# The last layer of a two-layer perceiver kernel: another split of the first block's convolution, its rows written by ScalarE's queue, and sums, gate product and closing addition at later places in the long last stage

## The reference

```python
# Mamba block, on x = layernorm(X) as tokens of 256 features; 512 inner channels, 16 states
xz = x @ in_proj_w.T + in_proj_b
x_main, z = split(xz, 2)
xc = silu(causal_conv(x_main, conv_w, 4 taps per channel) + conv_b)
ssm = xc @ x_proj_w.T + x_proj_b          # 33 rows: B (16), C (16), one step size
delta = softplus(ssm[..., -1:])
A = -exp(A_log)
for t in tokens:                          # per sequence, channel and state
    h = exp(A * dt) * h + dt * B_t * x_t
    y = sum_n(h * C_t) + D * x_t
y = (y * silu(z)) @ out_proj_w.T + out_proj_b
x = X + layernorm(y + x) * gamma + beta
# experts, on layernorm(x): the kernel adds all 8 experts, scaled by one gate value per token
out = (sum over experts of (gelu(xf @ w1 + b1) @ w2 + b2)) * norm_g
x = x + out
```

## Time and profile before

| what | value |
|---|---|
| median of 3 runs | 1706.67 us |
| lowest and highest | 1701.71 and 1714.98 us |
| profiled execution, its own time | 1697.53 us |
| its span, first to last instruction | 1695.7 us |
| busy over the span: TensorE, VectorE, ScalarE, GpSimd | 1370.2, 1219.3, 1073.7, 772.5 us |
| mean granted TensorE clock, share of full speed | 0.89 |
| transfers, all on SP's queue | 211.88 MB, mean 125 GB/s |

### The profile page before, as it was taken

How to read it: one execution, slowest core, us unless ns; L and a number is a source line. 1 busy time by engine, 2 the same in 40 slices (tenths; PEclk the granted TensorE clock), 3 DMA queues, 4 the chain that set the end, 5 groups by cost and what they waited for, 6 DMA issues and landing times. The chain is left out here.

```text
span 1695.7 us, 33885 instructions
## 1 busy us (share of the span) xinstructions
PE 1370.2 (81%) x12684; PEld 780.3 (46%) x12684; DVE 1219.3 (72%) x2296; ACT 1073.7 (63%) x1901; POOL 772.5 (46%) x842
## 2 busy tenths in 40 slices
PE   5999447978769977788884578995988889799898
PEld 4545224655544435555552222341444445345566
DVE  3599799972348866677765688999899899895200
ACT  2677345543354547777764367876998898794553
POOL 2355000000043434343440067766888788887443
PEclk9999767989869978789896789996999899899999
DMA  7497200000106656787741398787894475470000
GB/s 266 145 357 302 106 0 0 1 1 0 70 25 237 198 114 114 138 127 126 133 67 37 78 244 204 211 225 191 200 217 114 116 177 138 105 180 8 1 13 13
DMA packets 152695, 211.88 MB, mean 125 GB/s; under 512 B 107247, under 2 KB 112303, under 8 KB 139600
## 3 DMA queue, kind: packets, MB, share of 16 engines
q1 hardware_dynamic: 152532, 209.70, 47.9%
HBM read 154.85 MB, written 31.75 MB: 110 GB/s over the span
## 5 line engine op out<-in xcount | busy, mean ns | idle before, releaser
L2865 POOL TENSOR_TENSOR c_st<-c_st,c_c_rep 128x1024 f32<-128x1024 f32 x128 | 301.9, 2358 | 118.8 <-DVE c_st L2978 118.7
L2978 DVE TENSOR_TENSOR_SCAN c_st<-mf_dA,mf_u_ps 128x512 f32<-128x512 f32 x256 | 310.1, 1211 | 4.0 <-ACT mf_dA L3090 4.0
L2806 PE MATMUL mf_eh<-c_early,c_experts 128*128 128x512 f16 x768 | 196.3, 394 | 27.9 <-POOL c_early L2884 16.9
L2888 POOL TENSOR_TENSOR c_early<-c_early 128x512 f16<-128x512 f32 x128 | 148.5, 1161 | 108.9 <-ACT c_early L3107 108.7
L2827 PE MATMUL mf_ey<-c_experts,c_early 128*128 128x256 f16 x1536 | 192.8, 277 | 0.0
L2972 DVE TENSOR_TENSOR mf_u_ps<-c_st,mf_b_ps 128x512 f32<-128x512 f32 x256 | 177.6, 694 | 11.5 <-DVE c_st L2978 0.5
L2827 PEld LDWEIGHTS mf_ey<-c_experts,c_early 128*128 128x128 f16 x1536 | 152.3, 99 | 49.7 <-issue 5.0
L3090 ACT ACTIVATE mf_dA<-c_dt,c_neg_a 128x496 f32<-128x496 f32 x256 | 160.3, 697 | 0.7
L3104 ACT ACTIVATE c_early<-mf_eh,c_vecs 128x512 f16<-128x512 f32 x128 | 88.0, 688 | 106.7 <-PE mf_eh L2806 106.2
L2732 PE MATMUL mf_y_ps<-c_st,c_consts 128*32 128x512 f32 x512 | 107.3, 654 | 50.4 <-POOL c_st L2865 33.1
L259 POOL TENSOR_TENSOR c_parts<-mg_ln_hT,c_parts 128x512 f16<-128x512 f32 x8 | 9.1, 1157 | 296.8 <-ACT c_parts L250 296.8
(11 more groups left out here) (546 smaller groups left out, 2759.4 us busy)
## 6 DMA issues: line engine op xcount, KB each, us to landing
c_st<-xs SPq DMA_DIRECT2D x64, 1024.0 KB, 7.3
a_ctx_t<-in_ctx_t SPq DMA_DIRECT2D x16, 1024.0 KB, 9.1
a_ctx_n<-in_ctx_n SPq DMA_DIRECT2D x16, 1024.0 KB, 8.1
cqs<-a_whole_rows SPq DMA_DIRECT2D x16, 512.0 KB, 6.7
mo_raw<-in_l_w SPq DMA_DIRECT2D x16, 512.0 KB, 4.1
ws<-mo_split SPq DMA_DIRECT2D x32, 256.0 KB, 2.6
c_cq<-cqs SPq DMA_DIRECT2D x16, 512.0 KB, 5.1
c_experts<-ws SPq DMA_DIRECT2D x32, 256.0 KB, 7.7
```

The lines of the kernel that those rows point to most:

```text
L2806: m = e.matmul(bank("hidden", n)[:, :], w1[q][w][:, j, f * P:(f + 1) * P], parts[b % 2][x][:, j, :], start=(j == 0 and w + x == 0), stop=( ...
L2865: e.tensor_tensor(half(u, h), half(u, h), over(c_rep[u // UNITS % 2][:, :], [P, 2, BT], 1), ALU.mult).then_inc(hcs("done"), 1)
L2888: e.tensor_tensor(hid[n % HIDS][1][:, :], g[n % 2][:, :], hid[n % HIDS][0][:, :], ALU.subtract).then_inc(los("done"), 1)
L2978: e.tensor_tensor_scan(st[u % RING][:, j, :], dA[:, n % AHEAD, :], u_ps[j % 2][:, :], 0.0, ALU.mult, ALU.add).then_inc(hs("done"), 1)
```

## The change

In the inner stage:
- `ON_V` is 2. VectorE convolves tiles 0 and 1; TensorE convolves tile 3 into `conv_ps` and tile 2 into `row_ps`. The silus and the row products go in the order 0, 3, 1, 2 (`KEPT`). The sums of the rows go into `conv_ps`, the step column into `row_ps`, the spread steps into `conv_ps`.
- VectorE makes the diagonals of tiles 2 and 3 and normalises the other twelve tiles ahead of its convolutions; the copies of block 1's transposes move ahead of the short chain. TensorE's transposes of block 1 move ahead of its convolutions.
- ScalarE copies the first features ahead of the root of the other tiles, and takes an exponential of a dummy value after the last silu.
- ScalarE's queue stores the rows right behind the activation that keeps them, waits for them and fetches them back replicated, ahead of its wait for the spread steps. SP does none of this.
- The fetches of state tiles 1 to 3 are the first transfers of SP in the last stage.

In the last stage, for steps from 23 on: `sums` stands behind both pairs of hidden and combine; `finish` stands behind the third scan and not the first. In all steps `gate` stands behind the second `weigh`, and `final(b - 1)` stands behind the first scan of the step after (two tiles later).

```diff
--- before.py
+++ after.py
@@ -2251,7 +2251,8 @@
                 drain(n)
 
 
-ON_V = DC - 1
+ON_V = 2
+KEPT = (0, DC - 1, 1, ON_V)
 
 
 def l1_inner(nc, c):
@@ -2266,6 +2267,7 @@
         xn_ps = [ps(f"xn_ps{j}") for j in range(CJ)]
         in_ps = [ps(f"in_ps{q}") for q in range(DC)]
         conv_ps, row_ps = ps("conv_ps"), ps("row_ps")
+        sum_ps = conv_ps
         acc = [sb(f"acc{u}", [P, BT]) for u in range(ON_V)]
         lg, na, ez, wz, lz, dz, mz, step = (sb(f"dt_{k}", [P, KT_]) for k in
                                             ("lg", "na", "ez", "wz", "lz", "dz", "mz", "step"))
@@ -2293,12 +2295,6 @@
                 e.dma_start(c.d["xs"][0, :, :, j, :].rearrange("q r t -> r q t"), c.xc[T * j:T * j + T, :, :]).then_inc(x_out, 16)
             e.wait_ge(x_out, 4 * 16)
             fetch_states(e, c, 0)
-            e.wait_ge(rows_kept, 1)
-            e.dma_start(c.d["ssm"][:, 0:BT], c.ssm[0:2 * NS, :]).then_inc(ssm_out, 16)
-            e.wait_ge(ssm_out, 16)
-            replicate_rows(e, c, 0)
-            for u in range(1, RING):
-                fetch_states(e, c, u)
             e.wait_ge(loaded, 3 * 16)
 
         @block.gpsimd
@@ -2314,7 +2310,7 @@
                     if i == 1:
                         e.wait_ge(kept_rows, CJ)
                     elif i:
-                        e.wait_ge(xs, DC)
+                        e.wait_ge(xs, (i - 2) * CJ + j + 1)
                     to = turn_banks[(max(i - 1, 0)) * CJ + j]
                     for k in range(KT_):
                         t = e.transpose(to[:, k * P:(k + 1) * P], c.xn[:, i * KT_ + k, j * P:(j + 1) * P], c.ident[:, :])
@@ -2328,27 +2324,28 @@
                     m = e.matmul(in_ps[q][:, :], c.w_x[:, j, q * P:(q + 1) * P], c.hT[:, j, 0:BT],
                                  start=(j == 0), stop=(j == CJ - 1))
                 m.then_inc(x_t, 1)
-            e.wait_ge(diag_made, TAPS)
-            e.wait_ge(xs, DC)
-            for k in range(TAPS):
-                m = e.matmul(conv_ps[:, :], c.diag[:, ON_V * TAPS + k, :], c.xm[:, ON_V, :, k:k + T],
-                             start=(k == 0), stop=(k == TAPS - 1))
-            m.then_inc(conv_t, 1)
-            for q in range(DC):
-                at = (ON_V, 0, 1, 2)[q]
-                e.wait_ge(silus, q + 1)
-                m = e.matmul(row_ps[0:NR, :], c.w_rows[:, at, :], c.xc[:, at, :], start=(q == 0), stop=(q == DC - 1))
+            turn(1)
+            e.wait_ge(diag_made, (DC - ON_V) * TAPS)
+            for q, to in ((DC - 1, conv_ps), (ON_V, row_ps)):
+                e.wait_ge(xs, DC)
+                for k in range(TAPS):
+                    m = e.matmul(to[:, :], c.diag[:, q * TAPS + k, :], c.xm[:, q, :, k:k + T],
+                                 start=(k == 0), stop=(k == TAPS - 1))
+                m.then_inc(conv_t, 1)
+            for q, at in enumerate(KEPT):
+                e.wait_ge(silus, max(q + 1, 2))
+                m = e.matmul(sum_ps[0:NR, :], c.w_rows[:, at, :], c.xc[:, at, :], start=(q == 0), stop=(q == DC - 1))
             m.then_inc(rows_t, 1)
             e.wait_ge(rows_kept, 1)
             for k in range(KT_):
-                m = e.matmul(conv_ps[:, k:k + 1], c.ssm[2 * NS:NR, k * P:(k + 1) * P], c.ones[2 * NS:NR, 0:1],
+                m = e.matmul(row_ps[:, k:k + 1], c.ssm[2 * NS:NR, k * P:(k + 1) * P], c.ones[2 * NS:NR, 0:1],
                              start=True, stop=True)
             m.then_inc(lg_t, 1)
-            for i in range(1, BLOCKS):
+            for i in range(2, BLOCKS):
                 turn(i)
             e.wait_ge(stepped, 1)
             for k in range(KT_):
-                m = e.matmul(row_ps[:, k * P:(k + 1) * P], step[:, k:k + 1].broadcast_to([P, P]), c.ident[:, :],
+                m = e.matmul(conv_ps[:, k * P:(k + 1) * P], step[:, k:k + 1].broadcast_to([P, P]), c.ident[:, :],
                              start=True, stop=True)
             m.then_inc(spread, 1)
 
@@ -2389,19 +2386,26 @@
                         o = e.scalar_tensor_tensor(a, x, w, a, ALU.mult, ALU.add)
                         o.then_inc(*(own() if k < TAPS - 1 else (conv, 1)))
 
+            def copy_turned(i):
+                for j in range(CJ):
+                    e.wait_ge(turned, i * CJ + j + 1)
+                    e.tensor_copy(c.hT[:, j, i * BT:(i + 1) * BT], turn_banks[(i - 1) * CJ + j][:, :]).then_inc(moved, 1)
+
             first, others = list(range(KT_)), list(range(KT_, TILES))
             statistics(first)
             normalised(first, 1)
             statistics(others)
-            taps_of(ON_V)
+            for q in range(ON_V, DC):
+                taps_of(q)
+            normalised(others, 2)
             for q in range(ON_V):
                 convolve(q)
-            normalised(others, 2)
             e.wait_ge(ready, 1)
             e.tensor_scalar(c.neg_a[:, :], c.neg_a[:, :], -1.0, None, ALU.mult).then_inc(made, 1)
+            copy_turned(1)
             e.wait_ge(lg_kept, 1)
             e.scalar_tensor_tensor(na[:, :], lg[:, :], -1.0, lg[:, :], ALU.mult, ALU.min).then_inc(negated, 1)
-            for q in range(ON_V - 1):
+            for q in range(ON_V):
                 taps_of(q)
             e.wait_ge(exped, 1)
             e.tensor_scalar(wz[:, :], ez[:, :], 1.0, None, ALU.add).then_inc(summed, 1)
@@ -2420,11 +2424,8 @@
             e.tensor_tensor(lz[:, :], lz[:, :], ez[:, :], ALU.mult).then_inc(*own())
             e.wait_ge(*own.now())
             e.scalar_tensor_tensor(step[:, :], lg[:, :], 0.0, lz[:, :], ALU.max, ALU.add).then_inc(stepped, 1)
-            taps_of(ON_V - 1)
-            for i in range(1, BLOCKS):
-                for j in range(CJ):
-                    e.wait_ge(turned, i * CJ + j + 1)
-                    e.tensor_copy(c.hT[:, j, i * BT:(i + 1) * BT], turn_banks[(i - 1) * CJ + j][:, :]).then_inc(moved, 1)
+            for i in range(2, BLOCKS):
+                copy_turned(i)
             e.wait_ge(moved, (BLOCKS - 1) * CJ)
 
         @block.scalar
@@ -2439,30 +2440,37 @@
 
             e.activation(c.neg_a[:, :], c.vec["A_log"], ACT.Exp).then_inc(ready, 1)
             root(list(range(KT_)))
-            root(list(range(KT_, TILES)))
             for j in range(CJ):
                 e.wait_ge(turned, j + 1)
                 e.activation(c.hT[:, j, 0:BT], xn_ps[j][:, :], ACT.Copy).then_inc(kept_rows, 1)
+            root(list(range(KT_, TILES)))
             e.wait_ge(cleared, 1)
             for q in range(DC):
                 e.wait_ge(x_t, q + 1)
                 e.activation(c.xm[:, q, :, TAPS - 1:], by_batch(in_ps[q][:, :]), ACT.Identity,
                              bias=bias[:, q:q + 1]).then_inc(xs, 1)
-            e.wait_ge(conv_t, 1)
-            keep_conv(conv_ps, ON_V)
-            for q in range(ON_V):
-                e.wait_ge(conv, q + 1)
-                keep_conv(acc[q], q)
+            for q in KEPT:
+                if q < ON_V:
+                    e.wait_ge(conv, q + 1)
+                    keep_conv(acc[q], q)
+                else:
+                    e.wait_ge(conv_t, DC - q)
+                    keep_conv(conv_ps if q == DC - 1 else row_ps, q)
+            e.activation(ez[:, :], lx.std[:, 0:KT_], ACT.Exp, scale=-1.0)
             e.wait_ge(rows_t, 1)
-            e.activation(c.ssm[:, :], row_ps[0:NR, :], ACT.Identity, bias=c.sm["xp_b"]).then_inc(rows_kept, 1)
+            e.activation(c.ssm[:, :], sum_ps[0:NR, :], ACT.Identity, bias=c.sm["xp_b"]).then_inc(rows_kept, 1)
+            e.wait_ge(rows_kept, 1)
+            e.dma_start(c.d["ssm"][:, 0:BT], c.ssm[0:2 * NS, :]).then_inc(ssm_out, 16)
             e.wait_ge(lg_t, 1)
-            e.activation(lg[:, :], conv_ps[:, 0:KT_], ACT.Copy).then_inc(lg_kept, 1)
+            e.activation(lg[:, :], row_ps[:, 0:KT_], ACT.Copy).then_inc(lg_kept, 1)
             e.wait_ge(negated, 1)
             e.activation(ez[:, :], na[:, :], ACT.Exp).then_inc(exped, 1)
             e.wait_ge(summed, 1)
             e.activation(lz[:, :], wz[:, :], ACT.Ln).then_inc(logged, 1)
+            e.wait_ge(ssm_out, 16)
+            replicate_rows(e, c, 0)
             e.wait_ge(spread, 1)
-            e.activation(c.dt[:, 0:BT], row_ps[:, :], ACT.Copy).then_inc(dt_kept, 1)
+            e.activation(c.dt[:, 0:BT], conv_ps[:, :], ACT.Copy).then_inc(dt_kept, 1)
 
 
 RING, AHEAD, HIDS, LAG = 4, 10, 6, 3
@@ -2691,6 +2699,8 @@
                 e.wait_ge(*added.at("done", b * KT_ + KT_ - 1))
                 e.dma_start(c.d["out"][:, rows(b), :], c.X[:, rows(b), :]).then_inc(stored, 16)
 
+            for u in range(1, RING):
+                fetch_states(e, c, u)
             e.dma_start(w_out[:, :, :], c.d["l1_w_out"]).then_inc(w_loaded, 16)
             e.dma_start(wg[:, :, :], c.d["l1_wg"]).then_inc(w_loaded, 16)
             for s in range(SLOTS):
@@ -2837,7 +2847,7 @@
                     hidden(n)
                     if n >= LAG:
                         combine(n - LAG)
-                if 1 <= s <= N:
```

(11 more changed lines are left out.)

## The result

The changed kernel took 1696.47 us (median of 20 runs, 1687.21 to 1702.39), the kernel before 1701.95 (median of 20, 1697.28 to 1716.48): a ratio of 0.9947, 95% interval 0.9931 to 0.9964, or 9 us less (6 to 12). Forecast were 14.1 us less (a ratio of 0.9917), 1692.6 us against the 1706.67 of the first three runs.

A forecast was written before the change was run, and what follows sets the result against it. VectorE was taken to set the pace, SP's queue to end the inner stage and TensorE to set the end; 6 + 3.7 + 4.4 = 14.1 us less, 1692.6 us against the 1706.67 median, range 1680 to 1705.

The forecast's parts named there:

- main case: Whole kernel: the change does as told in all parts, 9 to 18 us gained; chance 0.48.
- Inner stage, 6 us: Inner stage: shorter chain and earlier row write bring VectorE's first last-stage multiply from 980.98 to 975, 6 us gained.
- Of 1.6 us only 0.9 is left: Inner stage, convolutions to row products: last silu 1.6 us earlier, but the sums of the rows only 0.9 us earlier.
- my two ends: Inner stage, ScalarE's row write: landing after between 3.9 us (fastest row) and 6.9 us.
- three moved fetches: Start of last stage: 3 MB of states fetched later, just covered; if not, a microsecond or two goes back.
- first rival: Inner stage: only the issue time is saved, 1.7 us there; sum 9.8, 1696.9 us; chance 0.12.
- Closing addition, 3.7 us: Last stage, VectorE: two more tiles done within its wait for the last combine, 3.7 us for the first addition.
- Sums, gate, end of the scans, 4.4 us: End of scans, TensorE: four pairs left after the last sums, not five; projection at 1558.8 instead of 1563.19, 4.4 us.
- I count it at nothing: Last stage, TensorE: sums waiting for the later finish cost nothing, up to 3.7 us a time if cover is gone.
- the chain behind it has no part that the change touches: Behind the last projection: norms, transposes and last 32 pairs are untouched, so the 4.4 us gain stays.
- second rival: Last stage gives nothing: ScalarE and GpSimd hold the pace, waits turn into waits for decays; 1700.7 us; chance 0.18.
- slower rival: Last stage: TensorE waits for the late finish and falls to the lower clock; 1730 us; chance 0.07.

The follow-up runs named there:

- e2: The kernel before with all edits of the last stage and none of the inner stage; ratio to before 1.0017 (0.9996 to 1.0038).
- e1: The kernel before with all inner-stage edits and the three state fetches moved, old last stage; ratio to before 0.9959 (0.9940 to 0.9978).
- e5: Changed kernel, but SP writes and replicates the rows, the write issued ahead of its wait for the state stores; ratio to before 0.9953.
- e8: Changed kernel plus 24 filler matmuls on TensorE around the last block's transposes and second combine; ratio to before 0.9935 (0.9910 to 0.9960).
- e9: Changed kernel, but sums late only in steps where no finish is waited for, finish at its old place, closing addition ahead of it; ratio to before 0.9961.
- e11: Kernel before with the new inner stage and the closing addition two tiles later, ahead of the finish; other last-stage order old; ratio to before 0.9965.
- e12: Changed kernel with one tile convolved on TensorE and three on VectorE, as before the change; ratio to before 0.9944 (0.9925 to 0.9963).
- e13: Combination: e12's inner stage, e11's last stage and e8's filler matmuls; ratio to before 0.9938 (0.9915 to 0.9962), 1693.54 us.
- e7: Changed kernel, but SP issues the three further state fetches in the inner stage, right behind the first; ratio to before 0.9994 (0.9971 to 1.0017).
- e6: Changed kernel, but SP writes and replicates the rows in the old place, behind state stores, wait and first state fetch; ratio to before 0.9968.
- e4: Kernel before with only sums behind both pairs, finish behind the third scan and gate behind the second weighing; ratio to before 1.0016.
- e3: Kernel before with only the closing addition moved two tiles later, behind the finish; ratio to before 1.0106 (1.0079 to 1.0133).

## Why the prediction was right or wrong

The sign was right, the time lies in the range of 1680 to 1705 us, and the inner stage did what was forecast. Of 14.1 us 9 came (6 to 12), so the size was too high, and the main case ("as told in all parts", with 9 to 18 us) did not come although 9 is its lower edge: the last stage, forecast at 8.1 us, gave nothing that can be seen (e2). That the time itself was missed by only 3.9 us is partly luck: 1692.6 starts from 1706.67, the median of three runs; from the later 1701.95 the same forecast would have been 1687.9.

- *Inner stage, 6 us.* Measured 7.2 in the profiled pair and 7 by the time of e1 (whose own profile has 6.2); eight profiles with the order of write and fetches as changed (e1, e5, e8, e9, e11, e12, e13 and the changed kernel's) have the first multiply 39.5 to 41.2 us after the start. The write was issued 28.4 us after it (forecast 28.8), the first multiply at 39.5 (forecast 40.8).
- *Its parts.* "Of 1.6 us only 0.9 is left" for the engines' order is near the 1.1 of this pair, but that is within the scatter of the profiles, and e12 gets it without the split. The sum behind it is uneven too: it takes 3.5 us for a convolution of 3.67 (measured 3.67 and 3.60), and counts all four row products from 958.5 on where it says that three of them start then. The write landed after 3.7 us, just under the lower of my two ends (3.9); the replicas, "3.9 us (up to 8)", took 6.7.
- *The three moved fetches.* I asked only whether they would come too late, not what they would do ahead of the replicas. e7: its first multiply comes 6.0 to 7.6 us later than in those eight profiles. This is the largest price that the prediction did not look at, and the change happened to avoid it.
- *The first rival, and the rule beside it.* The first multiply at 39.5 and not near 45 refutes the rival. The Trainium skill (DMA: Bandwidth & Descriptors, section Issuing engines are not separate DMA queues) says that a second issuing engine brings no second set of DMA engines. e5 and e7 agree: SP alone does as well, and ScalarE's replicas wait behind SP's fetches. What does not follow is the prediction's step from there to "this part would be worth the issue time alone", which it doubted itself: the new queue was also a new order, and the order of a blocked queue was worth 3.8 us (e6 against e5).
- *Closing addition, 3.7 us.* The mechanism came as told: waits down from 11.7 to 3.4, no new waits for decays. What failed is the step from "both waits still cover the 3.7" to 3.7 us of time. e11 takes away 11.5 us of these waits and gains nothing over e1. VectorE arrives earlier at the next thing that isn't ready: gate data, decays, sums.
- *Sums, gate, end of the scans, 4.4 us.* The projection stood 12.9 us earlier than before counted from the stage's start; forecast were 14.1. The stall and the six slow matmuls, which should have gone, were there again in another place. Yet e2 and e4 show no gain in time. Two steps did not hold. "I count it at nothing" for the sums' wait for the late finish: TensorE's waits for the finish rose by 12.4 us, and VectorE's finish waited 5.8 us for sums. What that costs isn't shown: in e9 TensorE waits only 11.9 us for the finish and VectorE not at all for sums, and it is no faster. The other step is "the chain behind it has no part that the change touches": it took 129.2 us before and in e1, and 131.8 to 135.0 in the seven kernels with all sums late and no fillers, down to a granted clock of 0.67 in the changed one. Old sums are no safeguard there, though: e11 took 130.8 and e3 134.8. On average the six profiles with the whole changed last stage and no fillers (the changed kernel, e2, e5, e6, e7, e12) have the projection 579.9 us after the first multiply and 133.9 us behind it, the two with the old one (before, e1) 583.0 and 129.2: some 3 us gained ahead of the projection and 4.7 lost behind it. In these profiles that leaves nothing.
- *The second rival* (last stage gives nothing, 1700.7 us against the median of then) is nearest to what came: e1 has the inner stage's gain and e2 none. Its mechanism, waits for decays, did not appear (2.0 against 4.0 us).
- *The slower rival* had the right place and far too high a price. Its clock is seen below.

**The clock, over all timed runs.** Mean granted clock of TensorE by kernel (standard errors 0.001): before 0.8888 to 0.8891 in the four sets of runs; old order of sums, e1 0.892, e11 0.891, e13 0.890; sums late only where no finish is waited for, e9 0.888; sums late in every step, changed kernel 0.884, e2 0.882, e4 0.882, e5 0.884, e6 0.884, e7 0.881, e8 0.883, e12 0.884. e3, with the old order, has 0.885. So kernels whose late sums wait for the finish have the lower clock, by 0.005 to 0.008 in the mean of 11 to 20 runs each, and it is no chance of one profile. What that costs in time over the whole kernel is not settled: it can't be separated from the waits that the same order takes away, and e9, which keeps the clock, is not faster.

**Left open.** How far one profile may be trusted for the last stage: with its code the same, the projection came between 576.6 and 586.0 us after the first multiply (changed kernel, e5, e6, e7, e12). Differences of 5 us there, mine of 5.6 among them, are inside this scatter; only the timed ratios count. The averages over six and two profiles above are a hint for the same reason, no proof. Nor is it known what makes the clock fall behind the projection in one kernel and not in another.

## What to carry to other kernels

Before moving a DMA to another queue, look at what its issue stands behind and at what stands ahead of its bytes: here the order was worth the gain and the queue nothing, and three megabytes fetched too early cost a 256 KB transfer seven microseconds. A wait removed from one of four engines, all 82 to 91% busy, was here found again under another name; count it as a gain only if the next thing needed is ready too. An operation placed behind one that waits for a DMA inherits that wait; as e3 and e11 have it, the same addition, ahead of or behind the finish, differed by some 18 us.
